# Causal attention stage: how the maximum's shift gets into the scores

## The reference

```python
qkv = nx @ Wqkv + bqkv                       # nx: layernorm of x, 112 x 256
scores = einsum('bqhd,bkhd->bhqk', q, k) / sqrt(16)   # 16 heads of 16
scores = where(causal, scores, finfo.min)
attn = softmax(scores, axis=-1)
out = einsum('bhqk,bkhd->bqhd', attn, v) @ Wo + bo
x = x + out; nx2 = layernorm(x)              # then gate and experts
```

## Time and profile before

| What | Value |
|---|---|
| Runs | 1993.32, 1999.8, 2001.38 us; median 1999.8 |
| Profiled execution | span 1993.9 us from first to last instruction; no separate device time is given for it |
| TensorE busy | 1902.1 us, 95% of the span |
| VectorE, ScalarE, GpSimd busy | 1352.1, 1082.1, 946.5 us |
| Causal stage | from about 515 to 850 us of the span |
| Old block L1071 | 512 matmuls of 32 x 112 by 32 x 112, median 257 ns each, overlapped |

### The profile page before, as it was taken

How to read it: one execution, slowest core, us unless ns; L and a number is a source line. 1 busy time by engine, 2 the same in 40 slices (tenths; PEclk the granted TensorE clock), 3 DMA queues, 4 the chain that set the end, 5 groups by cost and what they waited for, 6 DMA issues and landing times.

```text
span 1993.9 us, 60055 instructions
## 1 busy us (share of the span) xinstructions
PE 1902.1 (95%) x20383; PEld 1649.8 (83%) x20384; DVE 1352.1 (68%) x3326; ACT 1082.1 (54%) x2530; POOL 946.5 (47%) x1616
## 2 busy tenths in 40 slices
PE   7999999999799999799999999969999999999996
PEld 5888888887578888589999999968988888888885
DVE  6788878887368788653333333336888888888886
ACT  2555555555367777522223333337777777777773
POOL 4565566554246676600000000057776777677752
PEclk9999999999899999899999999989999999999999
DMA  8223322330180000111111111131111111111100
GB/s 233 89 86 90 111 86 86 114 107 14 38 291 27 23 27 23 54 63 37 37 35 36 34 37 37 37 100 38 41 35 39 34 39 34 39 34 39 34 15 10
DMA packets 98081, 118.86 MB, mean 60 GB/s; under 512 B 9442, under 2 KB 90466, under 8 KB 97890
## 3 DMA queue, kind: packets, MB, share of 16 engines
q1 hardware_dynamic: 91874, 103.32, 16.8%
q0 software_dynamic: 6144, 14.69, 2.5%
HBM read 67.26 MB, written 50.72 MB: 59 GB/s over the span
## 4 chain that ended last, share of the span: by engine, by line
PE 90%; DVE 4%; ACT 3%; issue 2%; POOL 1%; DMA 0%; DVEq 0%; ACTq 0%; POOLq 0%; SPq 0%
PE ps_quad L1382 11%; PE ps_out L1397 11%; PE ps_proj L179 9%; PE ps_quad L179 6%; PE ps_quad L530 5%; PE ps_quad L99 4%; PE ps_out L111 4%; PE ps_turned L105 4%; PE ps_out L538 3%; PE ps_quad L1806 3%; PE ps_turned L179 3%; PE ps_proj L1826 3%; PE ps_proj L614 2%; PE ps_turned L516 2%; PE ps_turned L1095 2%
## 5 line engine op out<-in xcount | busy, mean ns | idle before, releaser
L1301 ACT ACTIVATE e_act_T<-ps_quad,fc_b 128x128 f32<-128x128 f32 x504 | 136.8, 383 | 313.7 <-PE ps_quad L1382 313.7
L1382 PEld LDWEIGHTS ps_quad<-e_xT,e_w_now 128*128 128x128 f32 x2016 | 234.6, 192 | 7.6 <-DVE e_xT L1341 3.9
L1382 PE MATMUL ps_quad<-e_xT,e_w_now 128*128 128x128 f32 x2016 | 235.7, 275 | 3.4 <-DVE e_xT L1341 3.4
L1397 PE MATMUL ps_out<-w,e_act_T 128*128 x1008 | 228.1, 380 | 0.8 <-DVE e_y L1349 0.8
L1526 POOL MEMSET c_cT<- 128x2 f32 x2 | 0.1, 102 | 461.3 <-DMA c_wk<-in_L_xattn_Wk 461.3
L361 ACT ACTIVATE a_probsT<-ps_quad 125x1792 f32<-125x1792 f32 x96 | 159.8, 1665 | 101.1 <-PE ps_quad L530 101.1
L1397 PEld LDWEIGHTS ps_out<-w,e_act_T 128*128 128x128 f32 x1008 | 186.9, 190 | 23.7 <-issue 1.2
L1338 DVE COPY e_w_now<-w 128x2048 f32 (+1 forms) x63 | 77.3, 1227 | 190.0 <-PE ps_quad L1382 188.5
L131 ACT ACTIVATE c_probs<-ps_quad,c_negmax 112x375 f32<-112x375 f32 x256 | 143.6, 571 | 65.7 <-DVE c_negmax L116 65.7
L123 DVE TENSOR_SCALAR c_probs<-c_probs,c_recip 112x375 f32<-112x375 f32 x256 | 150.9, 630 | 4.5
L418 DVE TENSOR_REDUCE a_negmax<-ps_turned 112x2 f32<-112x750 f32 x128 | 120.1, 939 | 34.0 <-PE ps_turned L516 33.8
(11 more groups left out here) (344 smaller groups left out, 5463.4 us busy)
## 6 DMA issues: line engine op xcount, KB each, us to landing
slots<-a_zeros SPq DMA_DIRECT2D x60, 512.0 KB, 5.0
a_cT<-in_ctx_t SPq DMA_DIRECT2D x32, 375.0 KB, 3.6
c_cT<-in_ctx_t SPq DMA_DIRECT2D x32, 375.0 KB, 3.2
w<-in_fc_t SPq DMA_DIRECT2D x2, 4096.0 KB, 19.1
w<-in_fc_t SPq DMA_DIRECT2D x8, 1024.0 KB
e_xg<-slots SPq DMA_DIRECT2D x63, 128.0 KB, 2.0
slots<-e_y SPq DMA_DIRECT2D x63, 128.0 KB, 1.7
out<-c_fo SPq DMA_DIRECT2D x32, 112.0 KB, 1.9
```

The costliest lines, as they stand in the source:

```text
L1301: last = act.activation(act_T[par][:, c * TILE:(c + 1) * TILE], hidden[par][:, c // 4, (c % 4) * TILE:(c % 4 + 1) * TILE], ACT.Gelu, bias= ...
L1382: last = pe.matmul(hidden[par][:, c // 4, (c % 4) * TILE:(c % 4 + 1) * TILE], w1_now[:, k, c * 128:(c + 1) * 128], xT[par][:, k, :], start ...
L1397: last = pe.matmul(y_ps[:, 0:D], act_T[1 - par][:, c * TILE:(c + 1) * TILE], w2[:, bass.ds(e, 1), c, :].rearrange("p a d -> p (a d)"), sta ...
```

## The change

`shift` becomes [128, 4, 112]: ScalarE writes it in four activations, one for each h, each the whole transposed block times a 0/1 number for each partition (column h of a small `choice` [128, 5], one where p % 32 = h) with a bias of zero (its fifth column). So block h holds only the rows of head h. TensorE then needs, for each r, one matmul whose stationary operand is all ones, `whole` [128, 112], with 4 x 112 = 448 columns moving. The first waits for the last of the four activations. The load of `choice` shrinks, the conversion on ScalarE goes, VectorE fills `whole` once.

```diff
-        choice_raw = late[:, 0:4 * T].rearrange("p (h t) -> p h t", h=4)
...
-        negmax, shift, choice = sb("negmax", [T, 128]), sb("shift", [128, T], F32R), sb("choice", [128, 4, T], F32R)
+        negmax, shift, choice, whole = sb("negmax", [T, 128]), sb("shift", [128, 4, T], F32R), sb("choice", [128, 5]), sb("whole", [128, T], F32R)
...
-            (choice_raw, w["choice"]),
+            (choice[:, :], w["choice"]),
...
-                act.activation(choice[:, :, :], choice_raw, ACT.Copy).then_inc(cleared, 1)
...
-                        act.activation(shift[:, :], shift_out, ACT.Copy).then_inc(shift_ready, 1)
+                        for h in range(4):
+                            last = act.activation(shift[:, h, :], shift_out, ACT.Identity, scale=choice[:, h:h + 1], bias=choice[:, 4:5])
+                        last.then_inc(shift_ready, 1)
...
+                dve.memset(whole[:, :].bitcast(F32), 1.0)
...
-                dve.wait_ge(cleared, 2)
+                dve.wait_ge(cleared, 1)
...
-                        for h in range(4):
-                            for r in range(4):
-                                pe.matmul(quad[0:T, r, h * T:(h + 1) * T], choice[group(r), h, :], shift[group(r), :],
-                                          start=True, stop=False, skip_group_check=True)
+                        for r in range(4):
+                            pe.matmul(quad[0:T, r, 0:4 * T], whole[group(r), :], shift[group(r), :, :].rearrange("p h t -> p (h t)"),
+                                      start=True, stop=False, skip_group_check=True)
...
-    a["choice"] = np.broadcast_to((p[:, None] % 32 == np.arange(4)[None, :])[:, :, None], (128, 4, T)).astype(np.float32)
+    a["choice"] = (p[:, None] % 32 == np.arange(5)[None, :]).astype(np.float32) * (np.arange(5) < 4)
+    a["choice"] = a["choice"].astype(np.float32)
```

More of the change, by code:

```diff
@@ L1040, in _ @@
                 pe.wait_ge(weights_in, 16 * len(loads))
-                pe.wait_ge(cleared, 2)
+                pe.wait_ge(cleared, 1)
                 pe.wait_ge(wo_in, 16)
```

## The result

The changed kernel takes 2016.03 us (median of four runs, 2014.94 to 2018.4) against 2000.59 for the kernel before (median of four, the three shown above and one more): ratio 1.0082, 95% interval 1.0066 to 1.0097. It is slower by 15.4 us; 23 were forecast.

The account below looks back on a forecast made before the run. TensorE was taken to set the causal stage's pace, ScalarE close behind; 25 intervals x 0.81 = 20.3, plus 2.4, 1.2 and 0.1, together 24, less 1 for a stall: +23 on 1999.8, 2023 us, range 2009 to 2033.

Parts of the forecast that it names:

- ScalarE's copies: Causal stage, shift copy: four activations end at 1.46 us instead of 0.26, the instruction behind starts at 1.36 instead of 0.25.
- The pitch of L875: Start-to-start spacing of two-operand activations, 0.34 us, taken from the second-norm rows on ScalarE for the four new copies.
- TensorE's block: Choice-and-shift block on TensorE: four matmuls side by side take 0.30 us, saving 0.14, or 0.24 by the chain.
- The order of lateness: TensorE's later starts in a batch: ones block +0.53, output product +0.58, V product +0.89, gate product +0.81 us.
- the 1.11: Delay in us of all ScalarE work behind the copies (n2, kT, oT2, nn, q, q_high), none of it taken back.
- The sum: Whole kernel: 25 intervals growing 0.81 us each, 20.3, with edges 24, less 1 for the stall: +23 us.
- The first five intervals: Causal stage before the stall: the last three give 2.4 us, the first two 0.39 each.
- The stalled interval: One 14.89 us interval while expert weights load; could swallow about 3 us of gathered delay, 1 us taken off.
- shorter copies: Rival: the new copies' pitch is 0.25 us, not 0.34; +0.45 an interval, 2012 us; 15 in 100.
- the loop on ScalarE: Rival: ScalarE becomes the loop and nothing of the 1.11 us hides; 2032 us; 9 in 100, clock fall included.
- The row groups that do not run side by side: Rival: TensorE's four matmuls run one after another, block 0.85 us, +0.94 an interval, 2026 us; 5 in 100.
- a fall of the clock: Rival: TensorE's granted clock falls through the new waits; counted within the ScalarE loop's 9 in 100.

Follow-up runs that it names:

- e1: Kernel before plus three extra two-operand activations ahead of the shift copy, sixteen choice matmuls kept: interval 9.48 us, median 2011.6 us, ratio 1.0060.
- e6: Changed kernel with ScalarE's nn activation moved from behind oT2 to ahead of the shift copies: interval 9.52 us, median 2012.0 us, ratio 1.0066.
- e3: Kernel before with four 448-column matmuls of ones reading the single copied block four times, choice of rows left out: interval 8.93 us, median 1993.8 us, ratio 0.9973.
- e4: Changed kernel with TensorE's kT x qT first and the four matmuls of ones after it: interval 9.66 us, median 2013.6 us, ratio 1.0070.
- e2: Kernel before plus one extra two-operand activation ahead of the shift copy: interval 9.12 us, median 2001.6 us, ratio 1.0002.
- e7: Changed kernel with masking by one VectorE multiplication and no ScalarE shift copy, four matmuls kept: interval 9.15 us, median 1997.5 us, ratio 0.9997.
- e11: Changed kernel with scale-only copies, nn ahead of them, n2 behind kT and oT2, kT x qT before the ones block: 1993.8 us, ratio 0.9967.
- e5: Changed kernel with four Copy activations taking a scale and no bias, in place of Identity with both: interval 9.29 us, median 2002.1 us, ratio 1.0018.

## Why the prediction was right, and where its size was off

2023 us were forecast, with a range from 2009 to 2033, and 2016.0 measured. The mechanism is the forecast one: ScalarE's queue makes q_high, and oT2 ahead of it, come after TensorE needs them (the chain above, and e1 to e6).

- ScalarE's copies: 1.46 and 1.34 against 1.46 and 1.36. The pitch of L875 carried over. The estimate from the page "ScalarE: Activation LUTs" of the Trainium skill (section "What ACT_TABLE_LOAD costs") had put their end at 1.58.
- TensorE's block: 0.30 to the next block's start, as forecast. e3 shows its worth at 0.19 a batch, and e1 that in the changed kernel it is worth nothing. The row groups run beside each other: one matmul takes 454 ns and four of them 0.47. One small sum of the prediction does not come out: by the rule that it takes from the page "TensorE: Matmul & The Clock Gate" of the Trainium skill (Part 3, "Measured speedup vs the span model"), 448 columns at 2.4 per ns and three further tiles are an estimated 0.20, and with the 0.10 for the shape the same 0.30, not 0.02 less. Nothing rested on it.
- The order of lateness (ones block, output product for oT2, V product for q_high, gate product): right. e4 shows that the ones block's wait does not set the interval, and the chain above that in the changed kernel q_high does; oT2 is next, in e6, where q_high comes early.
- The step that was mis-sized is "None of these waited for its input before, so none can take the 1.11 back". kT did wait, for the key product (L1095). In the kernel before n2 started at 668.18 and kT only at 668.82, just behind the key product's end at 668.79:

```profile
667.73 1.06 PE L1095 MATMUL ps_proj<-s_nT,s_wqkv 128*128 128x112 f32 x8
...
668.82 0.60 ACT L848 ACTIVATE s_kT<-ps_proj,s_bqk 128x112 f32<-128x112 f32 x2
```

n2 and kT start 0.64 apart there and 0.49 in the changed kernel (668.57 and 669.06). The timeline shows no idle time on that row, for n2's 0.60 reaches almost to kT; the distance between the starts shows it. So 0.15 of the 1.11 was taken back and the term measured 0.96. n2 had waited a little too (last section), which moved nothing behind it. Another 0.09 is the stretch from the gate product to the values, 1.95 in the prediction and 1.86 measured. Together that is 0.24 of the 0.26 between 9.93 and 9.67.
- The sum: 25 x 0.55 = 13.8 in place of 20.3. The first five intervals gave 2.5 in place of 3.2 (2.4 and two of 0.39), but e2 has the same 2.5 without longer even intervals, so that this came out near is luck as much as reckoning.
- The stalled interval was 1.7 shorter, 1 had been taken off. That this was because of the delay is not shown: e2, with no delay, has 13.3 there, e7 15.5, e11 10.9, before 14.9. What sets it stays open.
- The rivals: shorter copies is what e5 built, and it gives 9.29, below the 9.57 put down for it by the same 0.24 and some; the loop on ScalarE did not come, with 25.0 us of waiting in 23 batches left ahead of the copies. The row groups that do not run side by side fall with the 0.30 of the block, a fall of the clock with its 1.00 from 600 to 845.

## What to carry to other kernels

On engines that execute in order, price an instruction by its successors: list when each result behind it is needed, and look along the path for what takes delay back. The smallest gap alone is too strict. Here it was q_high's: 0.22 us from its end and the wake to the V product. To it come 0.15 that kT gives back, 0.08 by which the V product was done ahead of the gate product (4.50 less 3.47 and 0.95), and the 0.09 behind the gate product. This sum, an estimate, is the 0.54 where the line of e5 meets 9.12. Four copies fitted in place of one once they had lost an operand and nn and n2 had been moved (e11). When measuring slack, compare start-to-start distances of neighbours with the same distance elsewhere, not only the idle times shown. A saving on the bounding engine is real only if the work that pays for it stays inside another engine's slack.

## What the runs showed of the hardware that was not expected

Copy with a scale in place of Identity with scale and bias took an fp32r-writing activation of 128x112 from 446 to 353 ns (medians) and the four of them from 1.46 to 1.09 us (e5, e11). The two edits, the operand left away and the other function, were not tried apart; Identity with one operand for each partition, L869, takes 380 ns.

The 0.25 us from the shift copy to n2 in the earlier trace rows is not what a plain copy costs. In e1 and e2 the next activation starts 0.14 behind the start of the plain copy in every batch. In the kernel before it is mostly 0.18 and 0.25 in turn, in e3 0.33 and 0.40, and in both kernels n2 starts 0.08 or 0.22 behind the end of GpSimd's last instruction for its rate (L763 before). So n2 waited for GpSimd there, too short a time to be shown as idle:

```profile
676.91 0.19 POOL L763 TENSOR_TENSOR s_o_shift<-s_minus,s_o_rate 112x1 f32<-112x1 f32 x1
...
677.19 0.60 ACT L843 ACTIVATE s_n<-s_y_rows,s_o_shift,s_o_rate 112x256 f32<-112x256 f32 x1
```
